# A graph layer's routing of edge tiles, moved from whole-array matmuls to pairs of 64-column tiles

## The chip, the cores and the metric

One NeuronCore of one Trainium2 chip runs the whole layer as one program. The metric is the device time of one execution in microseconds (us), lower is better. Before the change it is 1411.84 us, the median of two runs (1411.36 and 1412.31).

## What is computed

A message-passing layer over 6250 nodes of 64 features and 200000 edges that come sorted by their target node (`dst`) and carry random source nodes (`src`):

```
h   = relu(layernorm(x))
msg = relu(concat(h[dst], edge_attr) @ W1a + b1a) @ W1b + b1b     # per edge
agg = segment_sum(msg, src) / max(count(src), 1)                  # per node
out = x + relu(concat(h, agg) @ W2a + b2a) @ W2b + b2b
```

The costly part is the middle: a row of 64 numbers per edge has to be made, and then summed at the edge's source node, and the sources come in no order.

## The kernel before, in words

The kernel sums rows before W1b (which is linear), so that a sum is over 64 numbers and a count, per node. Every float32 row is split into three bf16 parts that add up to it, so that bf16 matmuls against matrices of zeros and ones sum exactly. A row with its count, its digits and the three parts is 196 columns wide (`RW`).

Edges go two ways. A "scattered" group is 6 tiles of 128 edges: TensorE combines equal sources within a tile (`combine`, L1578), ScalarE moves the result, and GpSimd adds the rows to tables in memory by indirect DMA (L651). A "dense" group is 8 tiles of 128 edges, and there are 115 of them (`DENSE`). The loop (`cycles`) has 120 steps, nearly all with one group of each kind; five dense groups make a "macro" group.

A dense group is summed in two stages:

1. **Routing** (`route`, L1589). The 6250 nodes are cut into 10 buckets. For each group VectorE builds `oh1` (`slots`, L1154): for every edge a row of 640 zeros and ones that says at which place the edge goes. The 8 tiles are two sides of 4 (`SIDES`, `SUB`). A bucket has 128 places per group: 64 (`PLACES`) for each side. One matmul takes 128 columns of `oh1` (places) as weights and 196 columns of rows as moving data; since a side fills 64 places of a bucket, 128 columns are *two buckets of one side*. Four matmuls, one per tile of the side, accumulate in PSUM. A "fill" is one PSUM bank with two such results; the table `FILLS` lists five fills of 8 matmuls for a group, which alternate between the two banks `l1_ps[0]` and `l1_ps[1]`.
2. **Node sums** (`sum_nodes`, L1603). Five groups later, each bucket of a macro group is summed into its 640 nodes with a second matrix of zeros and ones (`oh2`, made by VectorE at L1169): 15 matmuls of 64 or 65 columns per chunk, ten chunks in each step. VectorE adds the sums to the totals in SBUF (`add_sums`, L1176).

Between the stages ScalarE moves each fill from PSUM to `routed` in SBUF, as bf16 (`keep_routed`, L892). Because a bank holds 64 places of one bucket above 64 of another, a fill takes two instructions of 64 partitions; `bucket_at` says which bucket lies in which half (side 1 has them swapped, so that both sides of a bucket end in different halves).

Other work of a step: `z` (L1553 in float32, L1559 in bf16) makes the next groups' rows, `take_off` (L1566, 512 columns) takes a rounded part off so that ScalarE can round the rest (`split`, L869); in other groups VectorE does that (`split_dense`).

The order is written out by hand on each engine in `cycle`, and semaphores hold the engines together. On TensorE one step is: combine, z of both kinds, then five fills with the node sums of ten chunks between them. A fill waits until ScalarE has moved the fill two before it (`routed_ready`); the first waits for `oh1` (`slots_ready`).

Ahead of the loop the kernel makes h and its table, ranks the edges of each bucket (`rank_ps`, L1534, L1537), and GpSimd works out from the bucket an edge's first place (`place`, L635 to L645). A second way through the kernel (`general`), for inputs on which the places do not suffice, is not taken in the profiled run.

Of the kernel before, what the change touches and what calls it, by code (L numbers as in the profile page):

```python
# [22 lines left out]
ROWG = 1 + SIDES  # L23
# [4 lines left out]
BLOCKS = BUCKETS // SIDES  # L28
# [46 lines left out]
FILLS = (((0, 0), (0, 1)), ((0, 2), (0, 3)), ((1, 0), (0, 4)), ((1, 1), (1, 2)), ((1, 3), (1, 4)))  # L75
# [26 lines left out]
def done(n):  # L102

    return n + START


def bucket_at(side, block, half):

    return 2 * block + (half ^ side)
# [40 lines left out]
def gnn_kernel(nc, x, e_t, e_rows, src_col, dst_col, src_row, dst_row, weights, row_biases, out):  # L150
# [5 lines left out]
    with ExitStack() as ctx:  # L156
# [124 lines left out]
        assert TILES[DN] * RW + GE[DN] // 2 + DT <= NTP * D and COLS <= 5 * 2 * HALF  # L281
# [22 lines left out]
        WINDOWS = (SIDES, 1)  # L304
# [13 lines left out]
        dsidx = sb("dsidx", [P, TILES[DN]], i32)  # L318
# [115 lines left out]
        with nc.Block() as block:  # L434
# [140 lines left out]
            def _(pool):  # L575
# [51 lines left out]
                def low(b, m):  # L627
# [6 lines left out]
                halfway = [slice(k * SUB * DENSE, (k + 1) * SUB * DENSE) for k in range(SIDES)]  # L634
                nc.gpsimd.tensor_scalar(place[:, halfway[1]], bucket_b[:, halfway[1]], 0.5, -0.25, ALU.mult, ALU.add).then_inc(place_step, 1)  # L635
                nc.gpsimd.tensor_scalar(place[:, halfway[0]], bucket_b[:, halfway[0]], float(PLACES), 1.0, ALU.mult, ALU.add
                                        ).then_inc(place_step, 1)
                pool.wait_ge(place_step, 2)
                nc.gpsimd.tensor_scalar(place[:, halfway[1]], place[:, halfway[1]], SHIFT, SHIFT, ALU.add, ALU.subtract).then_inc(place_step, 1)
                pool.wait_ge(place_step, 3)  # L640
                nc.gpsimd.tensor_scalar(place[:, halfway[1]], place[:, halfway[1]], 4.0, None, ALU.mult).then_inc(place_step, 1)
                pool.wait_ge(place_step, 4)
                nc.gpsimd.tensor_tensor(place[:, halfway[1]], place[:, halfway[1]], bucket_b[:, halfway[1]], ALU.subtract).then_inc(place_step, 1)
                pool.wait_ge(place_step, 5)
                nc.gpsimd.tensor_scalar(place[:, halfway[1]], place[:, halfway[1]], float(PLACES), float(PLACES + 1), ALU.mult, ALU.add  # L645
                                        ).then_inc(place_step, 1)
# [81 lines left out]
                with pool.Else():  # L728
# [3 lines left out]
                    pool.wait_ge(ptab_out, 16 * len(P_PARTS))  # L732
                    pool.wait_ge(ids_out, 32)
# [9 lines left out]
                    def landed(scattered_groups, dense_groups):  # L743
                        return (scattered_groups * TILES[S] + dense_groups * TILES[DN]) // ANY_TABLES
# [8 lines left out]
                    def cycle(s, n, t, routes, sums_too):  # L753
# [11 lines left out]
                        if routes:  # L765
                            pool.wait_ge(dsidx_ready, done(t.value(1)))
                            scatter_any(DN, landed(s.base + n, routed_groups), dsidx[:], lambda k: dsame[:, k, 0:W])
# [28 lines left out]
            def _(act):  # L796
# [64 lines left out]
                def main(fit):  # L861
# [22 lines left out]
                    def keep_routed(t, f):  # L884

                        act.wait_ge(routing, done(t.times(len(FILLS), f + 1)))
                        bank = l1_ps[f % 2][:, 0:2 * RW].rearrange("p (i c) -> p i c", c=RW)
                        if fit:
                            for half in range(SIDES):
                                first, second = (bucket_at(side, block, half) for side, block in FILLS[f])  # L890
                                on = slice(half * PLACES, (half + 1) * PLACES)
                                ins = nc.scalar.activation(  # L892
                                    routed[on, t.div(MACRO).mod(2), first:second + 1:second - first, t.mod(MACRO), :], bank[on, :, :], ACT.Copy)
                            ins.then_inc(routed_ready, 1)
                            return
                        tiles = [side * SUB + block for side, block in FILLS[f] if block < SUB]
                        if f == 0:
                            act.wait_ge(dense_ended, done(t.value()))
                        if not tiles:
# [3 lines left out]
                        nc.scalar.activation(dsame[:, tiles[0]:tiles[-1] + 1, :], bank[:, 0:len(tiles), :], ACT.Copy).then_inc(routed_ready, 1)  # L903
# [54 lines left out]
            def _(dve):  # L958
# [15 lines left out]
                for kind in (S, DN):  # L974
# [3 lines left out]
                            (slice(1, ROWG), row_i[0][:, GE[DN]:ROWE].rearrange("p (r c) -> p r c", r=SIDES))]  # L978
# [91 lines left out]
                for b in range(BUCKETS):  # L1070
                    dve.wait_ge(ranks_raw, b + 1)
                    if b:
                        dve.wait_ge(ranks_kept, b)
                    chosen = masks[:, b, :, :].rearrange("p (s k) g -> p s (k g)", s=SIDES).bitcast(mybir.dt.uint16)
                    nc.vector.copy_predicated(pos.rearrange("p (s c) -> p s c", s=SIDES), chosen,
                                              rank_ps[b % 2][:, :, 0:SUB * DENSE]).then_inc(ranks_kept, 1)
# [190 lines left out]
                def fast():  # L1267
# [54 lines left out]
                    dve.wait_ge(place_step, 6)  # L1322
# [10 lines left out]
                def general():  # L1333
# [26 lines left out]
                    def dense_rows(t):  # L1360
# [6 lines left out]
                        nc.vector.scalar_tensor_tensor(out=dpick[:], in0=dsame[:, :, W], scalar=limit[:, 0:1],  # L1367
# [435 lines left out]
```

## Time and profile before

| | |
|---|---|
| median of two runs | 1411.84 us |
| profiled execution, first to last instruction | 1414.2 us |
| TensorE matmul busy | 1339.5 us, 95% |
| VectorE busy | 1341.4 us, 95% |
| ScalarE busy | 869.4 us, 61% |
| GpSimd busy | 1106.0 us, 78% |

The profile is one execution; its span is 2.4 us above the median of the runs, and no other time of that execution is given. Two engines are busy nearly all the time. A busy TensorE has to be read with care: matmuls overlap each other in the array, and a row's duration (193 ns for one of 64 columns) is much longer than the distance from one start to the next. What the array really costs is read from the starts of successive groups in the timeline.

### The profile page before, as it was taken

To read this page: it belongs to the slowest core of one execution; us is meant where nothing else is said; L and a number is where in the kernel's file an instruction comes from. 1 tells how busy PE (TensorE), PEld (TensorE's weight loads), DVE (VectorE), ACT (ScalarE), POOL (GpSimd) and SP (SyncE) were. 2 spreads that over 40 slices of the span, in tenths; PEclk is the share of its full clock that TensorE was granted. 3 is DMA by queue.
4 is the path that set the end of the run, shared out by engine and by line. 5 is a ranking of instruction groups with operands and counts; after the bars stand their busy time and mean duration, and the time that the engine had idled before them with its cause. 6 is when DMAs were issued, how large, how long until landed. Compare 5 with 4: busy or idle time off the path is not lost. (4 is left out here: it accounts for less than half of the span.)

```text
span 1414.2 us, 66554 instructions
## 1 busy us (share of the span) xinstructions
PE 1339.5 (95%) x27554; PEld 1298.9 (92%) x27554; DVE 1341.4 (95%) x4186; ACT 869.4 (61%) x1857; POOL 1106.0 (78%) x732
## 2 busy tenths in 40 slices
PE   4667999999999999999999999999999999999967
PEld 3556999999999999999999999999999999999965
DVE  7889999999999999999999999999999999999886
ACT  6246666666666666666666666666666666666505
POOL 3538888888888888887888878888788887888753
PEclk8779999999999999999999999999999999999988
DMA  4767767767777777776777767776677876777451
GB/s 153 303 145 142 120 116 124 123 116 128 125 123 128 116 124 122 123 128 122 119 121 130 129 112 121 127 128 127 108 122 128 125 134 101 125 126 123 64 154 48
DMA packets 225080, 178.60 MB, mean 126 GB/s; under 512 B 149632, under 2 KB 191742, under 8 KB 223751
## 3 DMA queue, kind: packets, MB, share of 16 engines
q1 hardware_dynamic: 130468, 145.66, 39.7%
q0 software_dynamic: 94304, 28.63, 28.5%
q8 instruction: 219, 3.59, 1.0%
q14 instruction: 89, 0.73, 0.2%
HBM read 140.88 MB, written 33.31 MB: 123 GB/s over the span
## 5 line engine op out<-in xcount | busy, mean ns | idle before, releaser
L651 POOL DMA_INDIRECT sums<-vv,sidx x648 | 1043.8, 1611 | 249.9 <-issue 185.7
L892 ACT ACTIVATE area<-rank_ps 64x392 bf16<-64x392 f32 x1150 | 563.7, 490 | 138.1 <-PE rank_ps L1589 114.0
L1603 PE MATMUL rank_ps<-area 128*128 128x65 bf16 x17250 | 614.6, 193 | 1.6 <-issue 1.6
L1603 PEld LDWEIGHTS rank_ps<-area 128*128 128x128 bf16 x17250 | 593.8, 98 | 11.0 <-issue 2.0
L1589 PE MATMUL rank_ps<-r_d,oh 128*128 128x196 bf16 x4600 | 497.6, 250 | 13.3 <-DVE oh L1154 5.3
L1589 PEld LDWEIGHTS rank_ps<-r_d,oh 128*128 128x128 bf16 x4600 | 381.5, 97 | 27.1 <-issue 7.7
L1169 DVE TENSOR_SCALAR area<-iota,local 128x640 bf16<-128x640 int16 x1150 | 397.4, 410 | 4.1
L1154 DVE TENSOR_SCALAR oh<-iota,rank 128x640 bf16<-128x640 int16 x920 | 312.3, 409 | 4.8 <-PE rank_ps L1589 3.7
L869 ACT ACTIVATE r_d<-z_ps 128x512 f32<-128x512 f32 x247 | 147.5, 597 | 81.5 <-PE z_ps L1559 77.9
L880 ACT ACTIVATE vv<-c_ps 128x396 f32<-128x396 f32 x108 | 54.1, 501 | 175.7 <-PE c_ps L1578 165.2
L1553 PE MATMUL z_ps<-wts,et_d 128*128 128x128 f32 x920 | 131.9, 287 | 1.1 <-ACT r_d L869 0.7
L1176 DVE TENSOR_TENSOR dense<-rank_ps,dense 128x325 f32<-128x325 f32 x230 | 111.6, 485 | 18.7 <-PE rank_ps L1603 18.1
L1122 DVE TENSOR_TENSOR r_s<-r_s 128x384 f32<-128x384 f32 x216 | 120.3, 557 | 4.8 <-ACT r_s L869 1.1
L1111 DVE TENSOR_SCALAR same<-ids_s,srcf 128x128 bf16<-128x128 int16 x648 | 118.3, 278 | 0.0
L1553 PEld LDWEIGHTS z_ps<-wts,et_d 128*128 128x128 f32 x920 | 112.8, 193 | 1.6 <-ACT r_d L869 1.0
L1553 PE MATMUL z_ps<-wts,et_s 128*128 128x128 f32 x648 | 99.4, 290 | 0.4 <-issue 0.4
L869 ACT ACTIVATE r_s<-z_ps 128x384 f32<-128x384 f32 x108 | 53.0, 491 | 69.1 <-PE z_ps L1559 69.1
L1553 PEld LDWEIGHTS z_ps<-wts,et_s 128*128 128x128 f32 x648 | 81.4, 193 | 0.5 <-issue 0.5
L1578 PE MATMUL c_ps<-r_s,same 128*128 128x64 bf16 (+1 forms) x1944 | 77.7, 193 | 1.4 <-issue 1.4
L1578 PEld LDWEIGHTS c_ps<-r_s,same 128*128 128x128 bf16 x1944 | 67.5, 97 | 1.5 <-issue 1.4
L1133 DVE TENSOR_TENSOR r_d<-r_d 128x512 f32<-128x512 f32 x98 | 67.1, 685 | 1.7
L1104 DVE TENSOR_SCALAR hots_s<-ids_s,basew 128x384 bf16<-128x384 int16 x216 | 65.5, 344 | 0.9 <-issue 0.8
(203 smaller groups left out, 794.8 us busy)
## 6 DMA issues: line engine op xcount, KB each, us to landing
ids_s<-ids SPq DMA_DIRECT2D x216, 192.0 KB
et_d<-in_e_t SPq DMA_DIRECT2D x115, 256.0 KB
ids_d<-ids SPq DMA_DIRECT2D x115, 256.0 KB
et_s<-in_e_t SPq DMA_DIRECT2D x108, 192.0 KB
sums<-vv,sidx POOLq DMA_INDIRECT x648
sums<-dense POOLq DMA_DIRECT2D x4, 1657.5 KB
wp_s<-p_table SPq DMA_DIRECT2D x216, 15.8 KB
wp_d<-p_table SPq DMA_DIRECT2D x115, 15.8 KB
```

The lines of the kernel that those rows point to most:

```text
L651: nc.gpsimd.indirect_dma_start(out=sums[t][:, :], out_offset=bass.IndirectOffsetOnAxis(ap=index, axis=0), in_=rows, in_offset=None, comput ...
L869: nc.scalar.activation(rows3(kind, g)[:, :, PARTS[r]:PARTS[r] + D], z, ACT.Relu).then_inc(split_ready[kind], 1)
L892: ins = nc.scalar.activation(routed[on, t.div(MACRO).mod(2), first:second + 1:second - first, t.mod(MACRO), :], bank[on, :, :], ACT.Copy)
L1111: ins = nc.vector.tensor_scalar(same[:, g.mod(2), k, :], ids_s[:, g.mod(SR), 0, k * P:(k + 1) * P], srcf[:, column_of(S, g, k):column_of(S ...
L1122: nc.vector.tensor_tensor(r3[S][:, :, PARTS[r + 1]:PARTS[r + 1] + D], r3[S][:, :, at:at + D], halves(S, g)[:, :, at:at + D], ALU.subtract) ...
L1154: ins = nc.vector.tensor_scalar(oh1[:, k, :], iota[:], pos[:, bass.ds(t.value(k * DENSE), 1)], None, ALU.is_equal)
L1169: nc.vector.tensor_scalar(oh2[:, g, :], iota[:], local[:, n.mod(2), g:g + 1], None, ALU.is_equal).then_inc(nodes_ready, 1)
L1176: nc.vector.tensor_tensor(part, l2_ps[h][:, 0:BW], part, ALU.add).then_inc(summed, 1)
L1553: nc.tensor.matmul(z_ps[kind][:, j * P:(j + 1) * P], et[kind][:, slot, j * P:(j + 1) * P], wts[:, C_W1A_BOT:C_W1A_BOT + P], start=j == 0, ...
L1578: t = nc.tensor.matmul(c_ps[b][:, k * R:k * R + n], same[:, b, k, :], halves(S, g)[:, k, PARTS[r]:PARTS[r] + n], start=r == 0, stop=r == 2)
L1589: ins = nc.tensor.matmul(l1_ps[f % 2][:, i * RW:(i + 1) * RW], oh1[:, k, block * P:(block + 1) * P], halves(DN, t)[:, k, :], start=k == si ...
L1603: ins = nc.tensor.matmul(l2_ps[h][:, u * W:u * W + w], oh2[:, g, u * P:(u + 1) * P], rows[:, PARTS[r]:PARTS[r] + w], start=g % MACRO == 0 ...
```

## The change

Routing's matmuls become half as wide and twice as many. Each takes 64 columns of `oh1` (the places of one bucket and one side) and writes 64 partitions of the bank: side 0 the lower, side 1 the upper ones. In the built program these 9200 matmuls run on array tiles of 128 rows by 64 columns, 4600 of them at column 0 and 4600 at column 64, alternating; all other matmuls keep the whole array of 128 by 128. A fill is now two whole buckets, so ScalarE moves it in one instruction of 128 partitions, and `bucket_at` goes. On TensorE fills 0 and 1 now follow each other, then 2 and 3, then 4 alone, with chunks 0 and 1, chunks 2 to 4, and chunks 5 to 9 of the node sums behind them. GpSimd's calculation of places, which put the buckets of side 1 in swapped order, is one instruction. The `general` way is adapted (smaller one-hot slices, an input `src_strips`, four scatters per tile); in the ranking ahead of the loop two loops are written differently and give the same instructions. The constants `WINDOWS_S` and `HALF_TILES` rename sizes that stay 2 and 4.

```
-FILLS = (((0, 0), (0, 1)), ((0, 2), (0, 3)), ((1, 0), (0, 4)), ((1, 1), (1, 2)), ((1, 3), (1, 4)))
+FILLS = tuple((b, b + 1) for b in range(0, BUCKETS, 2))
...
                 pool.wait_ge(lane_step, 7)
-                halfway = [slice(k * SUB * DENSE, (k + 1) * SUB * DENSE) for k in range(SIDES)]
...
+                nc.gpsimd.tensor_scalar(place, bucket_b, float(PLACES), 1.0, ALU.mult, ALU.add).then_inc(place_step, 1)
...
                         bank = l1_ps[f % 2][:, 0:2 * RW].rearrange("p (i c) -> p i c", c=RW)
+                        first, last = FILLS[f]
                         if fit:
-                            for half in range(SIDES):
-                                first, second = (bucket_at(side, block, half) for side, block in FILLS[f])
-                                on = slice(half * PLACES, (half + 1) * PLACES)
-                                ins = nc.scalar.activation(
-                                    routed[on, t.div(MACRO).mod(2), first:second + 1:second - first, t.mod(MACRO), :], bank[on, :, :], ACT.Copy)
-                            ins.then_inc(routed_ready, 1)
+                            nc.scalar.activation(routed[:, t.div(MACRO).mod(2), first:last + 1, t.mod(MACRO), :], bank,
+                                                 ACT.Copy).then_inc(routed_ready, 1)
                             return
...
                     pe.wait_ge(routed_ready, done(t.times(len(FILLS), max(0, f - 1))))
-                    for i, (side, block) in enumerate(FILLS[f]):
-                        for k in range(side * SUB, (side + 1) * SUB):
-                            ins = nc.tensor.matmul(l1_ps[f % 2][:, i * RW:(i + 1) * RW], oh1[:, k, block * P:(block + 1) * P],
-                                                   halves(DN, t)[:, k, :], start=k == side * SUB, stop=k == (side + 1) * SUB - 1)
+                    for i, bucket in enumerate(FILLS[f]):
+                        for k in range(SUB):
+                            for side in range(SIDES):
+                                strip = slice(side * PLACES, (side + 1) * PLACES)
+                                ins = nc.tensor.matmul(l1_ps[f % 2][strip, i * RW:(i + 1) * RW],
+                                                       oh1[:, side * SUB + k, bucket * PLACES:(bucket + 1) * PLACES],
+                                                       halves(DN, t)[:, side * SUB + k, :], start=k == 0, stop=k == SUB - 1)
                     ins.then_inc(routing, 1)
...
                         route(t, 0)
-                        sums_of(0)
                         route(t, 1)
+                        sums_of(0, 1)
                         if ahead and not on_vector(DN, t.plus(1)):
                             take_off(DN, t.plus(1), 0)
-                        sums_of(1)
                         route(t, 2)
-                        sums_of(2, 3)
+                        route(t, 3)
+                        sums_of(2, 3, 4)
                         if ahead and not on_vector(DN, t.plus(1)):
                             take_off(DN, t.plus(1), 1)
-                        route(t, 3)
-                        sums_of(4)
```

The program's order shows where this stands. On TensorE, at the head of a step in the middle of the loop, before (`et_s`, `et_d` are edge attributes, `wts` weights, `wp` and `hots` the near rows of the node table, `r_d` and `oh` the rows and `oh1`, `rank_ps` the PSUM banks of both stages, `area` the operands of the node sums; xN counts equal instructions, and a float32 matmul that stands once here has two records in the trace):

```order
L1553 MATMUL z_ps<-wts,et_s 128x128 x3
L1559 MATMUL z_ps<-wp_s,hots_s 128x64 x6
L1553 MATMUL z_ps<-wts,et_d 128x128 x4
L1559 MATMUL z_ps<-wp_d,hots_d 128x64 x8
L1589 MATMUL rank_ps<-r_d,oh 128x196 x8
L1603 MATMUL rank_ps<-area 128x65
L1603 MATMUL rank_ps<-area 128x64 x2
```

And the same place now:

```order
L1552 MATMUL z_ps<-wts,et_s 128x128 x3
L1558 MATMUL z_ps<-wp_s,hots_s 128x64 x6
L1552 MATMUL z_ps<-wts,et_d 128x128 x4
L1558 MATMUL z_ps<-wp_d,hots_d 128x64 x8
L1590 MATMUL rank_ps<-r_d,oh 64x196 x32
L1605 MATMUL rank_ps<-area 128x65
L1605 MATMUL rank_ps<-area 128x64 x2
```

Where 8 matmuls of 128 output partitions stood ahead of the first chunk of node sums, 32 of 64 partitions stand now (two fills of 16). Further on in a step with `take_off`, on TensorE, before:

```order
L1603 MATMUL rank_ps<-area 128x64 x2
L1589 MATMUL rank_ps<-r_d,oh 128x196 x8
L1566 MATMUL z_ps<-r_d,minus_b 128x512
L1603 MATMUL rank_ps<-area 128x65
L1603 MATMUL rank_ps<-area 128x64 x2
```

And now:

```order
L1605 MATMUL rank_ps<-area 128x65
L1605 MATMUL rank_ps<-area 128x64 x2
L1565 MATMUL z_ps<-r_d,minus_b 128x512
L1590 MATMUL rank_ps<-r_d,oh 64x196 x32
L1605 MATMUL rank_ps<-area 128x65
L1605 MATMUL rank_ps<-area 128x64 x2
```

The fill that stood ahead of `take_off` has gone to the head of the step, and `take_off` now stands between two chunks of node sums and a burst of two fills. Over the whole loop the routing had 550 runs of 8 matmuls and 5 of 40 (in the first five steps there are no node sums to stand between); it now has 220 runs of 32, 110 of 16 and 5 of 80. On ScalarE, one step of the loop before (`vv` is the scattered group's result):

```order
L880 ACTIVATE vv<-c_ps 128x396
L869 ACTIVATE r_s<-z_ps 128x6x64
L874 ACTIVATE r_d<-rank 128x8x2
L869 ACTIVATE r_d<-z_ps 128x8x64
L892 ACTIVATE area<-rank_ps 64x2x196 x4
L869 ACTIVATE r_d<-z_ps 128x8x64
L892 ACTIVATE area<-rank_ps 64x2x196 x4
L869 ACTIVATE r_d<-z_ps 128x8x64
L892 ACTIVATE area<-rank_ps 64x2x196 x2
```

And now:

```order
L869 ACTIVATE vv<-c_ps 128x396
L858 ACTIVATE r_s<-z_ps 128x6x64
L863 ACTIVATE r_d<-rank 128x8x2
L858 ACTIVATE r_d<-z_ps 128x8x64
L879 ACTIVATE area<-rank_ps 128x2x196 x2
L858 ACTIVATE r_d<-z_ps 128x8x64
L879 ACTIVATE area<-rank_ps 128x2x196 x2
L858 ACTIVATE r_d<-z_ps 128x8x64
L879 ACTIVATE area<-rank_ps 128x2x196
```

Ten moves of half a bank have become five of a whole one, at the same places between the other moves.

## Rows read from the trace of the kernel before

**Rows 1.** The page's head and part 1: busy us, share of span, instructions.
```profile
span 1414.2 us, 66554 instructions
PE 1339.5 (95%) x27554; PEld 1298.9 (92%) x27554; DVE 1341.4 (95%) x4186; ACT 869.4 (61%) x1857; POOL 1106.0 (78%) x732
```

**Rows 2.** Windows, steps with node sums: length, busy per engine (instructions), clock, DMA share, GB/s.
```profile
136.00:1338.00 1202.00, 1199.24 (x25769) 1178.04 (x25767) 1170.19 (x3728) 779.75 (x1649) 997.42 (x622) 1.00 0.72 120
```

**Rows 3.** Waits of TensorE, same window: us in total, times, longest.
```profile
PE rank_ps L1589 <- issue: 1.4, 2, 0.9
PE z_ps L1553 <- issue: 0.8, 2, 0.4
PE rank_ps L1603 <- issue: 0.3, 1, 0.3
```

**Rows 4.** Waits of VectorE, same window.
```profile
DVE dense L1176 <- PE rank_ps L1603: 14.1, 14, 1.8
DVE oh L1154 <- PE rank_ps L1589: 3.5, 17, 0.2
```

**Rows 5.** Timeline of TensorE, one step: start, us, engine, line, operation, count.
```profile
708.76 0.86 PE L1589 MATMUL rank_ps<-r_d,oh 128*128 128x196 bf16 x8
709.47 0.63 PE L1603 MATMUL rank_ps<-area 128*128 128x65 bf16 x15
709.93 0.86 PE L1589 MATMUL rank_ps<-r_d,oh 128*128 128x196 bf16 x8
...
714.56 2.43 PE L1603 MATMUL rank_ps<-area 128*128 128x65 bf16 x75
716.83 0.71 PE L1578 MATMUL c_ps<-r_s,same 128*128 128x66 bf16 x18
...
718.30 1.14 PE L1553 MATMUL z_ps<-wts,et_d 128*128 128x128 f32 x8
719.27 0.40 PE L1559 MATMUL z_ps<-wp_d,hots_d 128*128 128x64 bf16 x8
719.51 0.69 PE L1589 MATMUL rank_ps<-r_d,oh 128*128 128x196 bf16 x6
```

**Rows 6.** Timeline of TensorE at a `take_off`, in the step before.
```profile
701.71 0.39 PE L1566 MATMUL z_ps<-r_d,minus_b 128*128 128x512 bf16 x1
701.94 0.86 PE L1589 MATMUL rank_ps<-r_d,oh 128*128 128x196 bf16 x8
```

**Rows 7.** Groups of TensorE by form: busy us, mean ns, then idle before.
```profile
L1603 PE MATMUL rank_ps<-area 128*128 128x64 bf16 x11500 | 598.3, 193 | 1.4 <-issue 1.4
L1589 PE MATMUL rank_ps<-r_d,oh 128*128 128x196 bf16 x4600 | 497.6, 250 | 13.3 <-DVE oh L1154 5.3 <-issue 4.9 <-ACT area L892 1.7
```

**Rows 8.** Groups of weight loads by form.
```profile
L1589 PEld LDWEIGHTS rank_ps<-r_d,oh 128*128 128x128 bf16 x4600 | 381.5, 97 | 27.1 <-issue 7.7 <-ACT area L892 6.0 <-DVE oh L1154 3.8
L1553 PEld LDWEIGHTS z_ps<-wts,et_d 128*128 128x128 f32 x920 | 112.8, 193 | 1.6 <-ACT r_d L869 1.0 <-issue 0.6
```

**Rows 9.** Groups of ScalarE by form: the moves of routing.
```profile
L892 ACT ACTIVATE area<-rank_ps 64x392 bf16<-64x392 f32 x1150 | 563.7, 490 | 138.1 <-PE rank_ps L1589 114.0 <-issue 0.5
```

**Rows 10.** Waits of ScalarE, steps with node sums.
```profile
ACT vv L880 <- PE c_ps L1578: 163.7, 99, 2.3
ACT area L892 <- PE rank_ps L1589: 107.5, 269, 2.0
```

**Rows 11.** Timeline ahead of the loop: GpSimd's places and their reader on VectorE.
```profile
59.18 0.58 POOL L645 TENSOR_SCALAR rank<-rank 128x460 f32<-128x460 f32 x1
...
84.60 1.12 DVE L1323 TENSOR_TENSOR rank<-rank 128x920 f32<-128x920 f32 x1
```

**Rows 12.** Timeline of ScalarE in the first shown step.
```profile
708.96 0.60 ACT L869 ACTIVATE r_d<-z_ps 128x512 f32<-128x512 f32 x1 [0.61 <-PE z_ps L1559]
709.66 0.99 ACT L892 ACTIVATE area<-rank_ps 64x392 bf16<-64x392 f32 x2
```

More of the change, by code:

```diff
@@ L22 @@
 ROWE = GE[DN] + GE[S]
-ROWG = 1 + SIDES
+WINDOWS_S = 2
+ROWG = 1 + WINDOWS_S
 BUCKETS = 10
@@ L765, in cycle @@
                         if routes:
-                            pool.wait_ge(dsidx_ready, done(t.value(1)))
-                            scatter_any(DN, landed(s.base + n, routed_groups), dsidx[:], lambda k: dsame[:, k, 0:W])
+                            pool.wait_ge(dsidx_ready, done(t.times(STRIPS, STRIPS)))
+                            for strip in range(STRIPS):
+                                scatter_any(DN, landed(s.base + n, routed_groups) + strip * TILES[DN] // ANY_TABLES, dsidx[:, strip, :],
+                                            lambda k: dsame[:, k, 0:W])
                             for at in range(ANY_TABLES):
@@ L902, in keep_routed @@
                             return
[L903 removed]
+                        nc.scalar.activation(dsame[:, first:last + 1, :], bank, ACT.Copy).then_inc(routed_ready, 1)
                     def cycle(s, n, t, routes, sums_too):
@@ L1408, in general @@
                     dve.wait_ge(ptab_out, 16 * len(P_PARTS))
-                    step(nc.vector.tensor_scalar(src_td, srcf[:, 0:DT], untrash[:, 0:1], None, ALU.add))
+                    dve.wait_ge(dst_in, 32)
+                    step(nc.vector.tensor_scalar(src_td, src_td.bitcast(i32), untrash[:, 0:1], None, ALU.add))
+                    for strip in range(STRIPS):
+                        on = slice(strip * PLACES, (strip + 1) * PLACES)
+                        for j in range(STRIPS):
+                            step(nc.vector.tensor_scalar(strip_limit[on, j:j + 1], limit[on, 0:1], 2.0 ** (PLACES * (strip - j)), None,
+                                                         ALU.mult))
                     step(nc.vector.memset(basew[:], -1.0))
                     step(nc.vector.memset(oh1[:], 0.0))
-                    dve.wait_ge(place_step, 6)
+                    step(nc.vector.memset(dpick[:], 0.0))
+                    for strip in range(STRIPS):
+                        step(nc.vector.tensor_scalar(dsidx[:, strip, :], dpick[:], trash[:, 0:1], None, ALU.add))
+                    dve.wait_ge(place_step, 1)
                     step(nc.vector.memset(words(0, n_routed + n_oh2), 0.0))
@@ L1527, in _ @@
                         pe.wait_ge(ranks_kept, b - 1)
-                    for side, bank in enumerate((l2_ps[b % 2], l1_ps[b % 2])):
-                        mine = masks[:, b, side * SUB:(side + 1) * SUB, :]
-                        ranks = bank[:, 0:SUB * DENSE].rearrange("p (k g) -> p k g", k=SUB)
+                    for half, bank in enumerate((l2_ps[b % 2], l1_ps[b % 2])):
+                        mine = masks[:, b, half * HALF_TILES:(half + 1) * HALF_TILES, :]
+                        ranks = bank[:, 0:HALF_TILES * DENSE].rearrange("p (k g) -> p k g", k=HALF_TILES)
                         for r in range(TURNS):
@@ L1536, in _ @@
                         for before in range(1, SUB):
-                            ins = nc.tensor.matmul(ranks[:, before:SUB, :], ones_b[:], mine[:, 0:SUB - before, :], start=False, stop=True,
-                                                   skip_group_check=True)
+                            for first in range(0, HALF_TILES, SUB):
+                                ins = nc.tensor.matmul(ranks[:, first + before:first + SUB, :], ones_b[:],
+                                                       mine[:, first:first + SUB - before, :], start=False, stop=True,
+                                                       skip_group_check=True)
                     ins.then_inc(ranks_raw, 1)
```

61 lines of the change are left out of this document (27 added, 34 removed).

## The prediction

> **What bounds the kernel now.** I read the page's busy shares first: TensorE and VectorE at 95% each, ScalarE at 61% [rows 1]. Two nearly full engines do not say which one leads, so I cut out the steps that have both routing and node sums, 1202 us of the span, and asked there for busy time and for waits. TensorE has 1199.2 of 1202 us [rows 2] and in all that time waits 2.5 us, none of it for another engine [rows 3]. VectorE is idle for 1202 - 1170.2 = 31.8 us, and the waits that are named there, 14.1 and 3.5 us, are all for TensorE [rows 4]. So VectorE follows and TensorE leads, but VectorE follows closely: were TensorE shorter by more than about 32 us, VectorE would be the bound.
>
> A busy share of 99.8% does not prove that the array is full, since records overlap. The timeline of one step does [rows 5]. Take starts, not durations. Eight routing matmuls go from 708.76 to 709.47: 0.70 to 0.71 us, 87.5 ns each (other fills of that profile give the same). Fifteen node-sum matmuls go from 709.47 to 709.93: 0.46 us, 30 ns each; 75 from 714.56 to 716.83 in 2.27 us, again 30 ns. The step is 719.51 - 708.76 = 10.75 us, of which routing is 5 x 0.70 = 3.5 us and ten chunks of sums 10 x 0.456 = 4.6 us; combine and z fill the rest. One `take_off` moves 512 columns in 0.23 us, 0.45 ns a column [rows 6]; 196 columns at that rate are 88 ns. Routing therefore runs at the rate at which columns stream, and its weight loads, 97 ns each by their record [rows 8], are hidden entirely behind earlier matmuls. [...] Whatever the change adds to the array's time per step thus goes straight into the span, some 110 times.
>
> **The change, part by part.**
>
> *ScalarE's moves.* 1150 moves of 490 ns become 575 [rows 9]. The new ones have twice the partitions and the same 392 elements in each. I take 490 ns again, so 575 x 0.49 = 282 us of ScalarE go. None of that is on the path: ScalarE is idle 1202 - 780 = 422 us of the window [rows 2] and waits for TensorE, 163.7 us for `combine` and 107.5 us for these very fills [rows 10]. Worth nothing. If a move cost twice as much, ScalarE would be where it is now, so that is worth nothing either.
>
> *GpSimd's places.* The old calculation ends at 59.8 us, and VectorE reads it at 84.6 [rows 11]. The instructions that go save 25 us that nobody waits for: nothing. The other edits are constants of equal value or lie in the way that is not run.
>
> *Bursts.* Two fills in a row need both banks free. Fill 1 waits for nothing of its own step; fill 2 waits for the move of fill 0, fill 3 for that of fill 1. From the timeline: the burst starts at 0, ends at 1.4 us; chunks 0 and 1 end at 2.3; fill 3 starts at 3.0. ScalarE does one `split` (0.60 us, from 0.2 us after the head of the step) and starts its moves at 0.9 [rows 5, 12]; with 0.49 us each the move of fill 1 ends near 2.1. Fill 3 has 0.9 us to spare, and fill 4 more (fill 2's move ends about 3.7, fill 4 starts about 5.1). `take_off` comes later by one fill and the node sums of chunk 4 end at the same point as before (four fills and five chunks stand ahead of it in both orders), so VectorE's `add_sums` and, after fill 4, its `slots` find their operands when they did. No new wait; queued behind a late fill would be the rest of TensorE's step, so the cover matters, and it is there.
>
> *Pairs of half-width matmuls.* 4600 matmuls become 9200, 4600 pairs, each half with its own moving data of 196 columns. If the two halves run side by side, a pair takes what one whole matmul took, 87.5 ns, and routing costs 4600 x 87.5 ns = 402 us as now. If they run one after the other it is 805 us. Nothing can make a pair shorter than the streaming of its 196 columns, 88 ns by the `take_off` row. The trace has no tile narrower than 128 by 128, so both ends stay open. I take the lower one: the halves address different columns of the array and different partitions of PSUM, and two starts and two loads in 87.5 ns are no strain on a sequencer that issues a load and a matmul every 30 ns in the node sums. Some loss inside pairs, up to a tenth (4600 x 8.75 ns = 40 us), goes into the range.
>
> *Changes of the array's shape.* This is the term that decides. Before, every matmul of the loop is on 128 by 128. Now 110 steps have three bursts of narrow tiles between wide work and five steps have one, 335 bursts, and each is entered and left: 670 changes of shape. The trace shows none, so I bound one from rows. Below: nothing, if wide and narrow matmuls follow each other as closely as two wide kinds do now (z to routing to sums without a gap [rows 5]). Above: the array must be empty before the shape changes. A 64-column matmul lasts 193 ns where the next starts after 30, and a routing one 250 ns where the next starts after 87.5 [rows 5, 7]: in both, about 0.16 us of a matmul lies behind the point at which its successor normally starts. A full stop exposes that, and after it the first weight load too, 97 ns [rows 8], if it can't run ahead: 0.26 us. I take the middle value, 0.16 us, the rest of a matmul with the load hidden; it is the figure two independent rows give. 670 x 0.16 = 107 us.
>
> [...]
>
> *Sum.* 0 (ScalarE) + 0 (GpSimd) + 0 (bursts) + 0 (pairs) + 107 us: the profile's 1414.2 us would be 1521 us. The profiled span is 2.4 us above the median of the runs, so the time is 1411.8 + 107 = 1519 us, 7.6% slower.
>
> **The rivals.**
>
> *Forecast: pairs side by side, each change of shape paid.* With 0.05 to 0.26 us for a change (34 to 174 us) and 0 to 40 us inside pairs: 1446 to 1626 us. Chance 0.48.
>
> *Not slower: a change of shape costs nothing that can be seen.* Place: the 670 boundaries. If narrow loads and matmuls enter an array that still works on wide ones, the boundary costs no more than that from z to routing does today. It decides below 28 us in all (2% of 1412, about what a measurement of this kernel can tell from no change), 0.04 us a boundary. For it speaks that loads run ahead of earlier matmuls everywhere in the trace; against it, that in the trace a load always finds the same shape. Time 1412, up to 1440 us. Chance 0.16 within 2%. For better than that TensorE would have to fall, and the narrow tiles take away no column that streams; even then VectorE's 32 us of idle time are the floor, 1380 us. Chance 0.03.
>
> *Weight loads come to pace the pairs.* In routing each load now fills 64 columns, and a pair needs two. If such loads lose the pace of today's (one per 30 ns in the node sums) and run like the float32 ones, they set the pace: eight float32 records with loads of 193 ns take 0.97 us, 121 ns each for 128 columns [rows 5, 8]. Two loads of 64 columns at that rate are 121 ns for a pair, 33.5 ns more than now: 4600 x 33.5 = 154 us. Against it: those float32 matmuls may be slow by themselves. Time 1566 us without and 1673 us with the boundaries' 107. Chance 0.17.
>
> [...]
>
> *The two halves of a pair don't overlap.* 4600 x 87.5 = 402 us, 1814 us alone and 1921 us with the boundaries. For it: no row shows two matmuls streaming at once. Against it: the order alternates the strips, and nothing makes one half wait for the other. Chance 0.16.
>
> **How the numbers follow.** The time is the forecast's, 1519 us. The range runs from the not-slower case to the upper end of the load-paced one: 1405 to 1690 us; it leaves out the halves that don't overlap (0.16) and a gain (0.03). The forecast's own range is 1446 to 1626. Slower by over 2%: 0.48 + 0.17 + 0.16 = 0.81; within 2%: 0.16; faster: 0.03.
>
> **What would show each step right or wrong.** In the timeline of the changed kernel, a burst of 32 narrow matmuls should go from its first start to the next chunk's in 1.4 us plus one boundary: 1.4 says that boundaries are free, 1.5 to 1.7 is the forecast, 1.9 to 2.0 the load-paced rival, 2.8 and more no overlap. A burst of 16 against one of 32 parts the two terms: the difference is 16 narrow matmuls without any boundary, 0.70 us if pairs are side by side. Chunks of node sums should keep their 0.46 us of starts, except for a boundary at the first. ScalarE should fall to about 590 us busy with mean moves near 490 ns, VectorE keep its 1341 us and wait more for TensorE, mostly at `add_sums`. The forecast is wrong if TensorE waits for ScalarE's moves at the second fill of a burst, if narrow pairs come at another pace than 87.5 ns, or if the step, 10.75 us in the step shown, grows by less than 0.3 or more than 1.9 us.

## The result, and the profile after

The changed kernel takes 1488.3 us (median of two runs, 1487.8 and 1488.9) against 1411.8 us: ratio 1.0547, 95% interval 1.0516 to 1.0577. That is 76.5 us, or 5.5%, slower. The forecast was 1519 us, slower by 107 us, so the way, the mechanism and the range (1405 to 1690, the likeliest case 1446 to 1626) hold, and the size of one term was too large. The whole range is wide, for it takes in rivals as well; what tells the cases apart is the timeline below.

The page of the kernel after, its head and part 1 (busy us, share of the span, instructions; compare [rows 1]):

```profile
span 1486.0 us, 75174 instructions
PE 1414.0 (95%) x32154; PEld 1299.8 (87%) x32154; DVE 1333.8 (90%) x4186; ACT 605.0 (41%) x1282; POOL 1097.7 (74%) x727
```

The window that was used before, on the kernel after (as [rows 2]), and VectorE's longest waits over the whole span:

```profile
136.00:1338.00 1202.00, 1201.27 (x28434) 1109.97 (x28432) 1101.92 (x3534) 498.43 (x1040) 941.93 (x590) 1.00 0.67 116
```

```profile
DVE dense L1161 <- PE rank_ps L1605: 64.8, 72, 4.0
DVE oh L1139 <- PE rank_ps L1590: 35.0, 65, 0.6
```

TensorE is still full and its granted clock still 1.00. What has changed is VectorE, which has 100 us of this window idle instead of 32 and waits for TensorE at `add_sums` (L1161) and `slots` (L1139). ScalarE has fallen by 264 us over the span. The window now holds fewer steps of the same work, and of the busy engines only TensorE takes longer for a step.

The timeline of TensorE for one step after (start, us, engine, line, operation, count), to be set against [rows 5] and [rows 6]:

```profile
752.16 0.40 PE L1558 MATMUL z_ps<-wp_d,hots_d 128*128 128x64 bf16 x8
752.48 1.59 PE L1590 MATMUL rank_ps<-r_d,oh 128*64 128x196 bf16 x32
754.01 1.09 PE L1605 MATMUL rank_ps<-area 128*128 128x65 bf16 x30
754.93 0.39 PE L1565 MATMUL z_ps<-r_d,minus_b 128*128 128x512 bf16 x1
755.26 1.59 PE L1590 MATMUL rank_ps<-r_d,oh 128*64 128x196 bf16 x32
756.78 1.55 PE L1605 MATMUL rank_ps<-area 128*128 128x65 bf16 x45
758.17 0.39 PE L1565 MATMUL z_ps<-r_d,minus_b 128*128 128x512 bf16 x1
758.49 0.89 PE L1590 MATMUL rank_ps<-r_d,oh 128*64 128x196 bf16 x16
759.32 2.45 PE L1605 MATMUL rank_ps<-area 128*128 128x65 bf16 x75
```

Read starts again. "128*64" is the array tile. A burst of 32 narrow matmuls takes 754.01 - 752.48 = 1.53 us (and 756.78 - 755.26 = 1.52) to the next chunk's start, a burst of 16 takes 0.83. The difference of 16 narrow matmuls is 0.69 to 0.70 us, what 8 whole ones took: pairs stream side by side, 87 ns a pair, with no loss that this shows. What is left of a burst is 1.53 - 1.40 = 0.13 us for its beginning and the change back. The change on entering stands ahead of the burst: eight z matmuls took 0.24 us to the first routing matmul before [rows 5] and take 752.48 - 752.16 = 0.32 now; a `take_off` took 0.23 [rows 6] and takes 0.33. So a run of narrow matmuls costs 0.08 to 0.10 us on entering and 0.12 to 0.13 behind, about 0.215 us together. With 335 runs that is 72 us, nearly the whole of the 76.5. The spans of the two profiled executions differ by 71.8 us; the profile after has a span 1.8 us below its execution's time, while the one before has a span 2.4 us above the median of the runs, so by this estimate the execution profiled before was some 4 us longer than the median.

In the single records of the trace, the step from the last matmul of one shape to the first of the other is 123 ns behind a 64-column matmul on entering (29 to 30 ns without a change) and 321 behind one of 512 columns (231). On leaving it is 181 ns (87 to 88 from a whole routing matmul). So a change adds 90 to 94 ns to the step: 93 to 94 behind 64 columns, 90 behind 512, 93 to 94 behind a narrow routing matmul. In 97 of 100 pairs the two starts are 0 to 8 ns apart; the second pair of a burst comes 113 ns after the first instead of 87, once for each burst.

The weight loads show part of the reason. Without a change, a load's record starts 2 ns after the start of the matmul ahead of its own, so loads run one matmul ahead. At a change it starts 121 to 122 ns after that matmul's start on entering (320 behind 512 columns) and 176 on leaving, only 1 to 5 ns ahead of its own matmul. So across a change no load ran ahead in the steps with node sums, in 329 entries and 330 exits. The first narrow matmul then has a record of 274 ns instead of 248, which goes with the second pair's 25 ns.

The rows of weight loads and of ScalarE's moves after (busy us, mean ns; then idle before), against [rows 8] and [rows 9]:

```profile
L1590 PEld LDWEIGHTS rank_ps<-r_d,oh 128*64 128x64 bf16 x9200 | 394.6, 108 | 53.8 <-issue 38.7 <-DVE oh L1139 3.5
```

```profile
L879 ACT ACTIVATE area<-rank_ps 128x392 bf16<-128x392 f32 x575 | 285.8, 497 | 258.2 <-PE rank_ps L1590 246.9 <-issue 11.3
```

A load of 64 columns is recorded with 108 ns where one of 128 had 97, and a whole-bank move takes 497 ns where half a bank took 490.

### The profile page after: what moved, and what is told of

Same layout as the page of the kernel before. It is cut to its first block, busy times and chain, and to the rows that moved or that the text cites. A ratio compares the mean times of both kernels' runs of the same rounds, so it can differ in the third digit from the quotient of the medians.

```text
span 1486.0 us, 75174 instructions
## 1 busy us (share of the span) xinstructions
PE 1414.0 (95%) x32154; PEld 1299.8 (87%) x32154; DVE 1333.8 (90%) x4186; ACT 605.0 (41%) x1282; POOL 1097.7 (74%) x727
## 4 chain that ended last, share of the span: by engine, by line
PE 90%; DVE 4%; DMA 2%; issue 2%; POOL 1%; ACT 1%; SPq 0%; DVEq 0%; POOLq 0%
PE rank_ps L1605 38%; PE rank_ps L1590 29%; PE z_ps L1552 13%; PE c_ps L1577 4%; PE z_ps L1558 3%; PE z_ps L1565 2%; DMA ids<-ids_s 2%; DVE oh L1139 0%; DMA rowb<-in_row_biases 0%; DVE stage L1458 0%; DMA wp_s<-p_table 0%; POOL area L627 0%; DVE area L1443 0%; DVE same L1096 0%; DVE stat L1447 0%
## 5 line engine op out<-in xcount | busy, mean ns | idle before, releaser
L1605 PEld LDWEIGHTS rank_ps<-area 128*128 128x128 bf16 x17250 | 544.3, 98 | 54.4 <-issue 46.7
L1605 PE MATMUL rank_ps<-area 128*128 128x65 bf16 x17250 | 584.0, 194 | 2.8 <-issue 2.8
L1590 PE MATMUL rank_ps<-r_d,oh 128*64 128x196 bf16 x9200 | 471.3, 252 | 9.2 <-issue 5.9
L1590 PEld LDWEIGHTS rank_ps<-r_d,oh 128*64 128x64 bf16 x9200 | 394.6, 108 | 53.8 <-issue 38.7
L879 ACT ACTIVATE area<-rank_ps 128x392 bf16<-128x392 f32 x575 | 285.8, 497 | 258.2 <-PE rank_ps L1590 246.9
L1139 DVE TENSOR_SCALAR oh<-iota,rank 128x640 bf16<-128x640 int16 x920 | 313.4, 410 | 37.7 <-PE rank_ps L1590 35.0
L1161 DVE TENSOR_TENSOR dense<-rank_ps,dense 128x325 f32<-128x325 f32 x230 | 112.3, 488 | 65.1 <-PE rank_ps L1605 64.8
L1089 DVE TENSOR_SCALAR hots_s<-ids_s,basew 128x384 bf16<-128x384 int16 x216 | 61.2, 324 | 0.9 <-issue 0.8
```

The costliest lines, as they stand in the source:

```text
L879: nc.scalar.activation(routed[:, t.div(MACRO).mod(2), first:last + 1, t.mod(MACRO), :], bank, ACT.Copy).then_inc(routed_ready, 1)
L1139: ins = nc.vector.tensor_scalar(oh1[:, k, :], iota[:], pos[:, bass.ds(t.value(k * DENSE), 1)], None, ALU.is_equal)
L1161: nc.vector.tensor_tensor(part, l2_ps[h][:, 0:BW], part, ALU.add).then_inc(summed, 1)
L1590: ins = nc.tensor.matmul(l1_ps[f % 2][strip, i * RW:(i + 1) * RW], oh1[:, side * SUB + k, bucket * PLACES:(bucket + 1) * PLACES], halves(D ...
L1605: ins = nc.tensor.matmul(l2_ps[h][:, u * W:u * W + w], oh2[:, g, u * P:(u + 1) * P], rows[:, PARTS[r]:PARTS[r] + w], start=g % MACRO == 0 ...
```

## The experiments

The theory to be tested is the forecast's: what costs is the change of the array's shape, twice for each run of narrow matmuls, 0.215 us a run by the timeline. Its rivals are a loss inside the pairs, a loss by the bursts' order, weight loads that pace narrow matmuls, and ScalarE's moves giving something back. Where one run is given, there is no interval. The changed kernel ran again beside its variants.

> The changed kernel once more, beside its variants on one chip. Both theories: 1488 us, ratio to the kernel before about 1.054.

Measured 1487.75 us (1485.74 to 1488.22), ratio 1.0545 [1.0527, 1.0562], as at first.

**More runs of narrow matmuls: the old order.**

```
                         route(t, 0)
+                        sums_of(0)
                         route(t, 1)
-                        sums_of(0, 1)
...
+                        sums_of(1)
                         route(t, 2)
-                        route(t, 3)
-                        sums_of(2, 3, 4)
+                        sums_of(2, 3)
...
+                        route(t, 3)
+                        sums_of(4)
```

> The changed kernel with its narrow matmuls, but with the order of fills and node sums of the kernel before: 550 runs of 16 narrow matmuls and 5 of 80, where the changed kernel has 335 runs in all. Theory (a run costs for its two changes of shape, some 0.215 us by the changed kernel's timeline: 0.095 on entering, 0.025 at its second pair, 0.1 on leaving): 220 more runs, 220 x 0.215 = 47 us, so 1535 us. Rival A (the loss lies within the pairs, 76 us / 4600 = 17 ns each): no more pairs, so 1488 us. Rival B (the loss is what bursts of two fills cost against the old order): back to about 1412 us.

Measured 1534.45 us, ratio 1.0874 [1.0856, 1.0892]: 46.7 us more for 220 more runs, 0.212 us each. The loss goes with the number of runs; it is not in the pairs, of which there are as many, nor in the new order.

**Fewer runs: three fills, then two.**

```
                         route(t, 1)
-                        sums_of(0, 1)
+                        route(t, 2)
+                        sums_of(0, 1, 2)
...
-                        route(t, 2)
+                        sums_of(3, 4)
                         route(t, 3)
-                        sums_of(2, 3, 4)
-                        if ahead and not on_vector(DN, t.plus(1)):
-                            take_off(DN, t.plus(1), 1)
...
                         route(t, 4)
+                        if ahead and not on_vector(DN, t.plus(1)):
+                            take_off(DN, t.plus(1), 1)
```

> The changed kernel with two runs of narrow matmuls in a step instead of three (fills 0 to 2, then 3 and 4; node sums 0 to 4 between them with the first take_off, the second take_off behind fill 4): 225 runs instead of 335. Theory (cost per run, 0.215 us): 110 x 0.215 = 24 us less, 1464 us, if no fill waits for ScalarE; fill 2 then starts 1.4 us after fill 0 and the move of fill 0 ends about then, so up to 0.1 us a step (11 us) may come back. Rival A (loss within pairs): 1488 us. Rival B (longer bursts cost more): above 1488 us.

Measured 1472.46 us, ratio 1.0439 [1.0422, 1.0456]: 15.3 us less, not the 24 of the runs alone. The burst of 48 shows where the rest stayed (timeline of TensorE):

```profile
758.76 2.37 PE L1590 MATMUL rank_ps<-r_d,oh 128*64 128x196 bf16 x48
761.06 1.55 PE L1605 MATMUL rank_ps<-area 128*128 128x65 bf16 x45
```

It takes 2.30 us where 24 pairs at 87 ns and 0.13 us make 2.22. The records show where: in all 110 bursts of 48 the first pair of fill 2 comes some 142 ns after the pair before it instead of 87, and in 109 of them 51 to 53 ns after ScalarE's move of fill 0 has ended. The next pair comes 113 ns later instead of 87. That is 0.08 us a burst, 9 us in 110, which makes up the difference between 24 and 15.3. It is the wait of fill 2 for the move of fill 0 that the expectation had as "up to 11 us". In the changed kernel no fill waits so; fill 3 of a step starts at least 1.1 us after the move that it needs.

The late next pair stands here without a change of shape. Fill 2's first load starts only 2 ns ahead of its matmul, and that matmul's record is 274 ns long, as at the head of a burst. So the 25 ns go with a load that could not run ahead, whether a change of shape or a wait held it back.

**The new order without narrow tiles.**

```
                         route(t, 0)
-                        sums_of(0)
                         route(t, 1)
+                        sums_of(0, 1)
...
-                        sums_of(1)
                         route(t, 2)
-                        sums_of(2, 3)
+                        route(t, 3)
+                        sums_of(2, 3, 4)
...
-                        route(t, 3)
-                        sums_of(4)
```

> The kernel before with its whole-array matmuls and two moves a fill, but fills and node sums in the changed kernel's order (bursts of two, two and one). Theory (only changes of shape cost, and here are none): 1412 us, within 3 us of before. Rival B (the bursts cost): up to 1488 us.

Measured 1413.56 us, ratio 1.0018 [1.0007, 1.0030]. The order of the fills is worth about 2 us (1 to 4 by the interval); a burst of 16 whole-array matmuls between wide work costs next to nothing. So the shape costs, not the burst.

**ScalarE's moves in halves again.**

```
-                            nc.scalar.activation(routed[:, t.div(MACRO).mod(2), first:last + 1, t.mod(MACRO), :], bank,
-                                                 ACT.Copy).then_inc(routed_ready, 1)
+                            for half in range(SIDES):
+                                on = slice(half * PLACES, (half + 1) * PLACES)
+                                ins = nc.scalar.activation(routed[on, t.div(MACRO).mod(2), first:last + 1, t.mod(MACRO), :], bank[on, :, :],
+                                                           ACT.Copy)
+                            ins.then_inc(routed_ready, 1)
```

> The changed kernel, but ScalarE moves each fill in two instructions of 64 partitions again, 1150 instead of 575. Theory (ScalarE has hundreds of us to spare and its moves are done before they are needed): ScalarE some 280 us busier, time unchanged within 3 us of 1488. Rival (whole-bank moves give back part of what the narrow tiles cost): slower; a tenth of 282 us would be 28 us, 1516 us.

Measured 1487.23 us, ratio 1.0540 [1.0522, 1.0558], against 1487.75 with whole moves:

```profile
L881 ACT ACTIVATE area<-rank_ps 64x392 bf16<-64x392 f32 x1150 | 564.8, 491 | 139.3 <-PE rank_ps L1593 112.9 <-issue 6.4
```

ScalarE does 279 us more and the time stays the same. The saving that the narrow tiles make possible is worth nothing here (1487.23 against 1487.75 us).

**The strips not alternating.**

```
-                        for k in range(SUB):
-                            for side in range(SIDES):
+                        for side in range(SIDES):
+                            for k in range(SUB):
```

> The changed kernel, but the four matmuls of side 0 of a bucket come first and then the four of side 1, so that the strips no longer alternate. Same matmuls, same loads, same runs. Theory (two neighbours on different strips stream side by side, two on one strip follow each other): of eight matmuls only the fourth and fifth overlap, a bucket takes 7 x 87.5 instead of 4 x 87.5 ns, 1150 x 262 ns = 302 us more, 1790 us. Rival (narrow matmuls are simply twice as fast, in any order): 1488 us.

Measured 1496.39 us in one run: 8.6 us more, not 302. The expectation was wrong. The timeline:

```profile
757.49 1.62 PE L1590 MATMUL rank_ps<-r_d,oh 128*64 128x196 bf16 x32
759.04 1.08 PE L1605 MATMUL rank_ps<-area 128*128 128x65 bf16 x30
```

Thirty-two matmuls, four on one strip and then four on the other, take 1.55 us, where alternating ones took 1.53. Either a narrow matmul costs half in any order, or matmuls of the second strip start ahead of earlier ones of the first. The records start in pairs from the first one on, 11 to 37 ns apart, one pair each 87 ns; they don't name the strip. The next run tells the two apart.

**One strip alone.**

```
-                            for side in range(SIDES):
+                            for side in range(1):
```

> The changed kernel without the narrow matmuls of side 1: each fill takes 8 matmuls on the lower strip alone, and ScalarE moves the lower 64 partitions (half of the routed rows are left out, so that the sums lack them). Theory (one strip streams a column per tick like the whole array, and the pace of 44 ns a matmul comes from two strips at once): 87 ns from start to start, bursts as long as before, time unchanged near 1488 us, and the same loss of some 0.1 us at each change of shape. Rival (a narrow matmul simply costs half): 44 ns from start to start, 4600 x 44 = 201 us less on TensorE, the time falls to where VectorE leads, near 1395 us.

ScalarE's move is cut to the lower half as well. Measured 1479.74 us in one run, 8 us under the changed kernel. The timeline:

```profile
756.07 0.88 PE L1590 MATMUL rank_ps<-r_d,oh 128*64 128x196 bf16 x8
756.89 2.45 PE L1605 MATMUL rank_ps<-area 128*128 128x65 bf16 x75
...
761.96 1.58 PE L1590 MATMUL rank_ps<-r_d,oh 128*64 128x196 bf16 x16
763.48 1.09 PE L1605 MATMUL rank_ps<-area 128*128 128x65 bf16 x30
```

Half the matmuls take the same time: 8 more on one strip are 1.52 - 0.82 = 0.70 us, 87 ns each. A narrow matmul on one strip takes as long as a wide one did (87.5 ns), and the second strip rides along: bursts of 16 and 8 take 1.52 and 0.82 us to the next chunk here, those of 32 and 16 with both strips 1.53 and 0.83. Both changes of shape are still paid with one strip: the steps are 123 ns on entering and 180 to 181 on leaving. It follows for the run before, from its pace, that the engine had both strips busy although the program listed one after the other. Had every matmul waited for the start of the one listed ahead of it, those 32 would have overlapped only where the strip changes; with three slots of 87 ns for each four they would take some 2.2 us, an estimate from the rows above. They took 1.55 us, so over four matmuls with their loads the second strip was not held up behind the first. How the engine does that no run shows.

**Short streams, narrow and wide.** In routing, and in ScalarE's moves of it, 68 of 196 columns are left, once with narrow tiles and once with whole ones. The narrow one's edit in routing:

```
-                                ins = nc.tensor.matmul(l1_ps[f % 2][strip, i * RW:(i + 1) * RW],
+                                ins = nc.tensor.matmul(l1_ps[f % 2][strip, i * RW:i * RW + MID],
...
-                                                       halves(DN, t)[:, side * SUB + k, :], start=k == 0, stop=k == SUB - 1)
+                                                       halves(DN, t)[:, side * SUB + k, 0:MID], start=k == 0, stop=k == SUB - 1)
```

> The changed kernel with 68 of the 196 moving columns in routing (the other two parts of each row are neither routed nor moved, so that the sums lack them). Asked of the timeline, at what pace pairs go when streaming is short: 68 columns stream in about 31 ns. Theory (narrow weight loads are hidden at 196 columns and not far from the limit): pairs at 50 to 90 ns, paced by their loads. Rival (narrow loads are as cheap as the wide ones, 30 ns or less each and side by side): pairs at about 31 ns. The time falls to where VectorE leads, 1350 to 1400 us, in either case, unless pairs stay at 87 ns (1488 us).

> The kernel before with 68 of the 196 moving columns in routing (the other two parts of each row are neither routed nor moved). The pair to the narrow one: whole-array matmuls of 68 columns should go at 30 to 33 ns each, as the node sums do; the time should fall to where VectorE leads, between 1350 and 1400 us.

Measured 1395.5 us narrow and 1404.1 us wide, one run each. Timelines, narrow first:

```profile
752.72 0.71 PE L1590 MATMUL rank_ps<-r_d,oh 128*64 128x68 bf16 x32
753.36 1.55 PE L1605 MATMUL rank_ps<-area 128*128 128x65 bf16 x45
754.85 0.45 PE L1590 MATMUL rank_ps<-r_d,oh 128*64 128x68 bf16 x16
755.23 0.29 PE L1605 MATMUL rank_ps<-area 128*128 128x65 bf16 x4
```

```profile
758.49 0.41 PE L1589 MATMUL rank_ps<-r_d,oh 128*128 128x68 bf16 x8
758.74 0.61 PE L1603 MATMUL rank_ps<-area 128*128 128x65 bf16 x15
```

Sixteen narrow matmuls are 0.64 - 0.38 = 0.26 us, 32 ns a pair with two loads; eight wide ones 0.25 us, 31 ns each. Two loads of 64 columns fit into 32 ns: they are not slower than one of 128, and the rival in which loads pace the pairs falls, its 50 to 90 ns with it. The window of 1202 us (as [rows 2]), narrow first, has VectorE as the fuller engine in both:

```profile
136.00:1338.00 1202.00, 1078.46 (x30680) 1004.32 (x30678) 1175.99 (x3771) 375.08 (x1099) 997.53 (x629) 0.98 0.71 123
136.00:1338.00 1202.00, 1040.95 (x26139) 988.53 (x26139) 1176.67 (x3761) 543.92 (x1651) 997.33 (x626) 0.97 0.71 123
```

So far less routing on TensorE saves 8 to 16 us against the kernel before, and no more. That 1395 us is a floor is not shown: VectorE still has 26 us of the window idle.

**Everything behind z on narrow tiles.**

```
-                    nc.tensor.matmul(z_ps[kind][:, 0:TILES[kind] * D], minus_b[:], halves(kind, g)[:, :, PARTS[r]:PARTS[r] + D],
...
+                    for side in range(SIDES):
+                        strip = slice(side * PLACES, (side + 1) * PLACES)
+                        ins = nc.tensor.matmul(z_ps[kind][strip, 0:TILES[kind] * D], minus_b[:, strip],
...
-                            ins = nc.tensor.matmul(l2_ps[h][:, u * W:u * W + w], oh2[:, g, u * P:(u + 1) * P],
+                            for side in range(SIDES):
+                                strip = slice(side * PLACES, (side + 1) * PLACES)
+                                ins = nc.tensor.matmul(l2_ps[h][strip, u * W:u * W + w],
+                                                       oh2[:, g, u * P + side * PLACES:u * P + (side + 1) * PLACES],
```

> The changed kernel with the node sums and take_off on pairs of 64-column tiles as well, same results: from the first fill to the last node sum of a step all matmuls are narrow, only combine and z stay on the whole array. 17250 + 132 more pairs, but 120 runs of narrow matmuls instead of 335. Theory (only changes of shape cost; pairs of 65 columns go at 31 ns as the short routing did): 120 x 0.215 = 26 us over the kernel before, about 1438 us. Rival (each narrow pair carries a small loss): pairs of 65 columns at, say, 5 ns more would cost 17250 x 5 = 86 us, so 1520 us or more.

Measured 1812.2 us, ratio 1.2825 [1.2797, 1.2852]. The theory had said 1438 us. The rival had said 1520 us or more, but for a loss of some 5 ns in each pair, and the timeline has 32 ns a pair, about 1 ns more than the 31 expected. The timeline and TensorE's longest wait:

```profile
755.18 1.11 PE L1610 MATMUL rank_ps<-area 128*64 128x65 bf16 x60
756.13 0.40 PE L1567 MATMUL z_ps<-r_d,minus_b 128*64 128x512 bf16 x2
756.36 1.86 PE L1593 MATMUL rank_ps<-r_d,oh 128*64 128x196 bf16 x32
...
760.41 0.35 PE L1610 MATMUL rank_ps<-area 128*64 128x65 bf16 x11
762.69 2.22 PE L1610 MATMUL rank_ps<-area 128*64 128x64 bf16 x128 [1.94 <-issue]
766.44 0.35 PE L1610 MATMUL rank_ps<-area 128*64 128x65 bf16 x11 [1.53 <-issue]
```

```profile
PE rank_ps L1610 <- issue: 239.7, 182, 3.9
```

The theory's own part is right: between node sums and `take_off`, and from `take_off` to routing (0.23 us again), the changes of line without a change of shape cost nothing, and 30 pairs of 65 columns take 0.95 us, 32 ns each. But TensorE stands still again and again, for 1.6 us in the middle of the cases, waiting for nothing that the profile shows, 240 us in 182 waits ahead of node sums alone. Counted over the trace, pauses of more than 0.7 us in the loop lie 256, 512 or 768 of TensorE's records (loads, matmuls and its semaphore instructions) apart, nearly without exception. The queue that brings instructions, before, in the changed kernel and here (packets, MB, share of the DMA engines' time):

```profile
q8 instruction: 219, 3.59, 1.0%
q8 instruction: 254, 4.16, 1.2%
q8 instruction: 390, 6.39, 1.4%
```

Its packets have 16 KB each, and their number is that of TensorE's records divided by 256, to within one: 56007, 65207 and 99971 records make 218.8, 254.7 and 390.5. I read from this that one packet brings a block of 256 of TensorE's instructions, and that the pauses stand where a new block is needed. At four instructions in 32 ns 256 of them last 2 us, in the node sums before (two in 30 ns) 4 us.

In the trace the pauses go with the landing of these packets. There are 183 pauses of more than 0.7 us at one place in the 256 records, 295 us in sum, and every one ends 1.2 to 1.7 us after a packet of this queue has landed. In the changed kernel the packets land 1.4 us or more, in the middle 3.4 us, before TensorE comes to that place, and there are no such pauses before 1409 us. The short narrow run has 36 of them, 49 us in sum. So the block comes too late, by this reading; no run changed the supply of blocks, and what of the 374 us over the forecast of 1438 lies outside these 295 is not traced.

No variant that does all of the work beat the kernel before. Among the narrow ones of them the best is the one with two runs a step, 1472 us.

## Why the prediction was right, step by step

- **TensorE leads, and what is added to it goes into the span.** Right. The window is as full as it was, and VectorE took the idle time.
- **ScalarE's moves worth nothing.** Right, and shown by the moves in halves: 279 us of ScalarE for no time. The 490 ns were 497.
- **GpSimd's places worth nothing.** Routing starts at 90.3 us in both traces, so nothing ahead of the loop changed.
- **Bursts of two wait for nothing.** Right; the wide kernel in that order is about 2 us slower. The working gave fill 3 0.9 us to spare; in the trace it is 1.1 to 1.4 us. With three fills in a row the margin is gone, and fill 2 waits.
- **Pairs at 87.5 ns.** Right, 87 to 88 ns by the records, and the halves do stream at once, as forecast: one strip alone takes as long, 1.52 us a burst against 1.53. The prediction used the alternating order as an argument for this, and the experiment's expectation made it a condition; there it was wrong.
- **Changes of the array's shape, 670 of 0.16 us.** This is the term that was mis-sized. The count is right and the cost is there, but it is 0.212 us for a run, 0.106 for a change; 670 x 0.106 = 71 us instead of 107. I had taken the rest of a matmul's record behind its successor's normal start, 0.16 us, for the time that the array needs to empty. The step between shapes exposes 90 to 94 ns, no more behind 512 columns (90) than behind 64 (93 to 94). The record's end is modelled, so the 0.16 us was no measure. I had also taken the next load as hidden, and it is not: it starts 1 to 5 ns ahead of its matmul, and some 25 ns at the head of a burst go with that. One part was too large and the other left out, so that the middle of a wide bracket (0.05 to 0.26 us) came so near is partly luck. What the 90 to 94 ns are made of stays open; no run separates that.
- **The rivals.** Free boundaries: out, by the count of runs. Loads that pace the pairs: out, by the short streams. Halves that don't overlap: out, by the one strip.
- **The signs.** A burst of 32 takes 1.52 to 1.53 us, at the low end of the forecast's 1.5 to 1.7. A step grows by some 0.6 us in the mean (71.8 us over 115 dense groups), inside the 0.3 to 1.9.

## What to carry to other kernels

Splitting a matmul that already fills the array's columns into strips gained no time on TensorE here: 87 ns a pair, as for the whole matmul. Where one strip was worked alone, the second one's columns stood empty, and filling them added 0.01 us to a burst of 1.52. Whether the split pays where the engine that empties PSUM is the bound is not shown; here that engine had 400 us to spare. If narrow tiles are wanted, count the runs of equal shape: each cost about 0.21 us here, where TensorE is full. Weigh a run saved against a wait for PSUM: three fills in a row waited 0.08 us and were still the better order. And count instructions: with 4 of them in 32 ns in the node sums TensorE paused for 295 us in all, which is not seen at 4 in 87 ns.

## What the runs showed of the hardware that was not expected

- Matmuls for two column strips ran side by side even when four for one strip were listed ahead of four for the other: 1.55 us for 32, against 1.53 alternating.
- Two loads of 64 columns went into 32 ns, where one of 128 columns went into 31, although their records are longer (108 against 97 ns in the full-length routing).
- A change of the array's shape added 90 to 94 ns to the step from start to start in each direction, 93 to 94 behind 64 columns and 90 behind 512. No weight load ran ahead across it (it started 1 to 5 ns ahead of its matmul), and the second narrow pair came 25 ns late (113 ns instead of 87), as it did after a wait without a change.
- With 4 instructions in 32 ns TensorE paused at distances of multiples of 256 records, 183 times for 295 us in all, each time until 1.2 to 1.7 us after a packet of 16 KB of the instruction queue had landed.
